# Two pair layers of a 512 x 512 x 128 tensor on one core: three stages of the second layer reordered or repacked

## What is computed

```python
xn = _layernorm(x, ln1_w, ln1_b)
p = _linear(xn, pi_w, pi_b)
g = jax.nn.sigmoid(_linear(xn, gi_w, gi_b))
h = p * g * mask[..., None]
a1, b1, a2, b2 = jnp.split(h, 4, axis=-1)
x1 = jnp.einsum('bikd,bjkd->bijd', a1, b1)
x2 = jnp.einsum('bkid,bkjd->bijd', a2, b2)
y = jnp.concatenate([x1, x2], axis=-1)
yn = _layernorm(y, ln2_w, ln2_b)
return _linear(yn, po_w, po_b) * jax.nn.sigmoid(_linear(yn, go_w, go_b))
```

## Time and profile before

| | us |
|---|---|
| median of the runs | 6269.43 |
| profiled execution | 6311.94 |
| its span on the core | 6310.3 |
| stage 4, about 1860 to 2775 of the span | 915 |
| stage 5, about 2775 to 4150 | 1375 |
| stage 6, about 4150 to 5259 | 1109 |
| stage 7, 5259.9 to the end | 1050 |

### The profile page before, as it was taken

How to read it: one execution, slowest core, us unless ns; L and a number is a source line. 1 busy time by engine, 2 the same in 40 slices (tenths; PEclk the granted TensorE clock), 3 DMA queues, 4 the chain that set the end, 5 groups by cost and what they waited for, 6 DMA issues and landing times. The chain is left out here.

```text
span 6310.3 us, 102506 instructions
## 1 busy us (share of the span) xinstructions
PE 4668.6 (74%) x29248; PEld 2698.7 (43%) x29248; DVE 4518.2 (72%) x6294; ACT 3638.4 (58%) x5197; POOL 2859.0 (45%) x1817
## 2 busy tenths in 40 slices
PE   0016656557539999968888888878887776999999
PEld 0015555543215555544444444445542233555554
DVE  5877767763657777777777777756666666777777
ACT  0017777762227766656666666645554455777777
POOL 0003333320017777756666666642223323666666
PEclk9998888988769999989999999999998888999999
DMA  7967777878739999977777777665555546999998
GB/s 295 366 226 174 187 172 175 181 177 285 242 128 348 345 343 339 342 252 251 249 249 249 247 250 249 238 213 199 199 195 185 180 160 227 326 324 327 325 325 307
DMA packets 991497, 1585.60 MB, mean 251 GB/s; under 512 B 40608, under 2 KB 403040, under 8 KB 988896
## 3 DMA queue, kind: packets, MB, share of 16 engines
q1 hardware_dynamic: 851488, 1398.78, 69.2%
q10 hardware_dynamic: 135680, 167.79, 7.3%
q0 software_dynamic: 4160, 16.78, 0.8%
HBM read 1060.48 MB, written 522.72 MB: 251 GB/s over the span
## 5 line engine op out<-in xcount | busy, mean ns | idle before, releaser
L1231 PE MATMUL s_y_ps<-s_ab 128*128 128x512 f16 x3072 | 747.4, 402 | 200.6 <-DVE s_ab L1287 142.7
L1509 POOL TENSOR_TENSOR s_oT<-s_gated,s_x1t 128x512 f32<-128x512 f32 x512 | 650.9, 1271 | 489.2 <-DVE s_gated L1438 487.3
L410 POOL TENSOR_TENSOR s_low<-s_xh,s_high 128x512 f16<-128x512 f32 x256 | 344.6, 1346 | 1042.4 <-DVE s_high L406 1042.4
L937 POOL TENSOR_TENSOR s_low<-s_xc,s_high 128x1024 f16<-128x1024 f32 x256 | 546.0, 2133 | 516.6 <-ACT s_high L900 516.1
L799 POOL TENSOR_TENSOR s_x1T<-s_gz,s_xT 128x512 f32<-128x512 f32 x512 | 650.2, 1270 | 233.4 <-DVE s_gz L765 231.2
L368 PE MATMUL s_turned_ps<-k_ident,s_xt 128*128 128x128 f32 x2048 | 366.1, 310 | 296.7 <-DMA s_xt<-in_x 259.1
L1231 PEld LDWEIGHTS s_y_ps<-s_ab 128*128 128x128 f16 x3072 | 309.9, 103 | 593.8 <-issue 278.5
L1008 DVE SCALAR_TENSOR_TENSOR s_h<-s_p_ps,k_pi_bias,s_gate 128x1024 f32<-128x1024 f32 x256 | 328.3, 1283 | 306.9 <-ACT s_gate L905 287.2
L706 PE MATMUL s_g_ps<-s_xT,s_Wg 128*128 128x512 f32 x1024 | 523.8, 593 | 0.0
L765 DVE SCALAR_TENSOR_TENSOR s_gz<-s_z_ps,k_z_bias,s_g 128x512 f32<-128x512 f32 x512 | 384.5, 751 | 192.3 <-ACT s_g L732 190.0
L900 ACT ACTIVATE s_high<-s_xc 128x1024 f16<-128x1024 f32 x256 | 270.6, 1057 | 420.1 <-DVE s_xc L1001 419.9
(11 more groups left out here) (209 smaller groups left out, 12712.4 us busy)
## 6 DMA issues: line engine op xcount, KB each, us to landing
s_xt<-in_x SPq DMA_DIRECT2D x512, 512.0 KB, 11.1
x_d<-s_x1T SPq DMA_DIRECT2D x128, 1024.0 KB, 9.1
s_xt<-x_d SPq DMA_DIRECT2D x128, 1024.0 KB, 8.3
h_d<-s_h SPq DMA_DIRECT2D x128, 1024.0 KB, 6.4
s_x1t<-x_d SPq DMA_DIRECT2D x256, 512.0 KB, 5.3
out<-s_ot ACTq DMA_DIRECT2D x256, 512.0 KB, 5.5
s_bt<-b_d SPq DMA_DIRECT2D x64, 1024.0 KB, 9.9
s_mask_b<-mask_d SPq DMA_DIRECT2D x128, 512.0 KB, 4.3
```

What stands on the lines that cost most here:

```text
L410: engine.tensor_tensor(low[:, u % 8, :], xh[:, u % 4, :], high[:, u % 8, :], ALU.subtract).then_inc(rest_ready[u % 2], 1)
L937: pool.tensor_tensor(low[:, n % 4, :, :], xc[:, n % 4, :, :], high[:, n % 4, :, :], ALU.subtract).then_inc(rest_ready, 1)
L1231: last = pe.matmul(y_ps[:, ib, 0:N], ab[:, u % 2, 0, a, kb, ib * P:(ib + 1) * P], ab[:, u % 2, 1, b, kb, :], start=m == 0, stop=m == len(t ...
L1509: pool.tensor_tensor(oT[:, row % 4, :], gated[:, row % 2, :], x1t[:, row // 2, row % 2, :], ALU.add).then_inc(added, 1)
```

## The change

In stage 5 ScalarE applies the sigmoid of pair n before it rounds pair n+2. In stage 6 the units are dealt out by a table, SLOTS, and stand ahead of the copy and the total of their quarter; the square and its sum of a quarter move behind the units of the next quarter; and the closing computation is cut into four pieces of 512 columns that pass between DVE and ACT, with two float16 parts where there were three bfloat16 ones. In stage 7 a row pair is the unit of everything: each of the two rows is multiplied from its own 64 partitions with 64-row weights, the two interleaved and written to two PSUM banks; gate, mix and addition take 1024 columns in one instruction; loads of x1 and stores move four rows; loads run up to 16 rows ahead; the spread runs four pairs ahead.

```diff
-                    for e in range(2):
-                        own, other = slice(64 * e, 64 * e + 64), slice(64 - 64 * e, 128 - 64 * e)
-                        dve.memset(w[other, :, e, :], 0.0)
...
+                    dve.tensor_copy(w[:, 0, :], wide[:]).then_inc(rounded, 1)
...
                 def step(r, n, last=False):
+                    open_gate(r, n)
                     if not (last and n + 2 >= PAIRS):
                         round_high(r, n + 2)
-                    open_gate(r, n)
...
+    SLOTS = (((), (0, 1, 2, 3), (4, 5, 6), (7,)), ((0,), (1,), (2, 3), ()))
...
-                        if after[0] == 0:
-                            turn(*after, 2 * ib)
-                            turn(*after, 2 * ib + 1)
+                        if after[0] == 0 and ib + 1 < RB:
+                            for v in SLOTS[0][ib + 1]:
+                                turn(*after, v)
...
+                        if after[0] < 2:
+                            for v in SLOTS[after[0]][ib]:
+                                round_high(*after, v)
+                        if ib:
+                            square(n - 1, ib - 1)
                         act.wait_ge(product, n)
                         act.activation(y[:, u, ib, :], y_ps[:, ib, 0:N], ACT.Copy).then_inc(copied, 1)
-                        if after[0] < 2:
-                            for v in range(ib * UNITS[after[0]] // RB, (ib + 1) * UNITS[after[0]] // RB):
-                                round_high(*after, v)
-                        act.wait_ge(summed, n)
-                        act.activation(y_ps[:, ib, 0:N], y_ps[:, ib, 0:N], ACT.Square).then_inc(squared, 1)
+                    square(n, RB - 1)
...
+                        if after[0] < 2:
+                            for v in SLOTS[after[0]][ib]:
+                                rest(*after, v)
+                        if ib:
+                            add_square(n - 1, ib - 1)
                         dve.wait_ge(copied, n)
                         dve.tensor_tensor(total[:, ib, :], total[:, ib, :], y_ps[:, ib, 0:N], ALU.add).then_inc(summed, 1)
...
+                    add_square(n, RB - 1)
...
-                step(dve.reciprocal(total[:], total2[:]))
...
+                    dve.reciprocal(total[:, ib, :], y[:, 1, ib, :]).then_inc(inverted, 1)
...
+                def product(dst, weights, n):
+
+                    for w, part, first, last in ((0, high, True, False), (1, high, False, False), (0, low, False, True)):
+                        for e in range(2):
+                            own = slice(64 * e, 64 * e + 64)
+                            done = pe.matmul(dst[:, e, 0:N], weights[own, w, :], part[own, n % 4, :], start=first, stop=last)
+                    return done
+
+                def project(r, n):
+                    pe.wait_ge(rest_ready, r * PAIRS + (n + 5))
+                    pe.wait_ge(sig, r * PAIRS + (n + 1))
+                    product(g_ps, K.Wgo, n).then_inc(g_done, 1)
+                    pe.wait_ge(mixed, r * PAIRS + (n + 2))
+                    product(p_ps, K.Wpo, n).then_inc(p_done, 1)
...
+                    if not (last and n + 4 >= PAIRS):
+                        scale(r, n + 4)
+                    if not (last and n + 2 >= PAIRS):
+                        mix(r, n + 2)
+                    if not (last and n + 4 >= PAIRS):
+                        rest(r, n + 4)
```

More of the change, by code:

```diff
@@ L1403, in step @@
-                def step(r, row, last=False):
-                    if row % 2 == 0 and not (last and row // 2 + 2 >= PAIRS):
-                        spread_scale(r, row // 2 + 2)
-                    if not (last and row + 2 >= ROWS):
-                        project(r, row + 2)
-                    turn(r, row)
-                spread_scale(0, 0)
-                spread_scale(0, 1)
+                    pe.wait_ge(scaled, r * PAIRS + (n + 1))
+                    pe.matmul(r_ps[:, n % 2, 0:N], K.halves[:], rt[:, n // 2, n % 2, :], start=True, stop=True).then_inc(spread, 1)
@@ L1413, in _ @@
+                for n in range(4):
+                    spread_scale(0, n)
                 project(0, 0)
                 project(0, 1)
[L1415 to L1419 removed]
+                with pe.Fori(0, REPS - 1) as r:
+                    for n in range(PAIRS):
+                        step(r, n)
@@ L1441, in step, with mix @@
-                def step(r, row, last=False):
-                    mix(r, row)
-                    if not (last and row // 2 + 2 >= PAIRS):
-                        (rest if row % 2 else scale)(r, row // 2 + 2)
-                for n in range(2):
+                    dve.tensor_tensor(low[:, n % 4, :], yn[:, n % 4, :], high[:, n % 4, :], ALU.subtract).then_inc(rest_ready, 1)
+                def mix(r, n):
+                    dve.wait_ge(sig, r * PAIRS + (n + 2))
+                    dve.wait_ge(p_done, r * PAIRS + (n + 5))
+                    dve.wait_ge(added, r * PAIRS + (n + 1))
+                    dve.scalar_tensor_tensor(gated[:, n % 4, :, :], p_ps[:], K.po_bias[:], gate[:, n % 2, :, :],
+                                             ALU.add, ALU.mult).then_inc(mixed, 1)
@@ L1447, in _, with step @@
+                def step(r, n, last=False):
+                    if not (last and n + 4 >= PAIRS):
+                        scale(r, n + 4)
+                    if not (last and n + 2 >= PAIRS):
+                        mix(r, n + 2)
+                    if not (last and n + 4 >= PAIRS):
+                        rest(r, n + 4)
+                for n in (0, 2):
                     scale(0, n)
+                    scale(0, n + 1)
                     rest(0, n)
-                with dve.Fori(0, N // ROWS - 1) as r:
-                    for row in range(ROWS):
-                        step(r, row)
@@ new lines, in open_gate, with keep @@
+                def open_gate(r, n):
+                    act.wait_ge(g_done, r * PAIRS + (n + 1))
+                    act.wait_ge(mixed, r * PAIRS + (n + 1))
+                    act.activation(gate[:, n % 2, :, :], g_ps[:], ACT.Sigmoid, bias=K.go_bias[:]).then_inc(sig, 1)
+                def keep(r, n):
+                    if n % 2 == 0:
+                        act.wait_ge(stored[n // 2], r * 16 + 16)
+                    for j in range(2):
+                        act.wait_ge(turned, r * (2 * PAIRS) + (2 * n + j + 9))
+                        act.activation(ot[:, n // 2, 2 * (n % 2) + j, :, :], o_ps[:, j, 0:N].rearrange("p (q c) -> p q c", c=P),
+                                       ACT.Identity).then_inc(kept, 1)
@@ new lines, in store, with step @@
+                def store(r, k):
+                    act.wait_ge(kept, r * (2 * PAIRS) + (U * k + U + 2))
+                    act.dma_start(out_v[:, bass.ds(r * (2 * PAIRS) + U * k, U)], ot[:, k, :, :, :]).then_inc(stored[k], 16)
+                def step(r, n, last=False):
+                    if not (last and n + 2 >= PAIRS):
+                        open_gate(r, n + 2)
+                    if not (last and n + 4 >= PAIRS):
+                        round_high(r, n + 4)
+                    keep(r, n)
+                    if n % 2 == 1:
+                        store(r, n // 2)
@@ new lines, in _ @@
+                with pool.Fori(0, REPS) as r:
+                    for n in range(PAIRS):
+                        if n % 2 == 0:
+                            pool.wait_ge(x_loaded[n // 2], r * 16 + 16)
+                        pool.wait_ge(mixed, r * PAIRS + (n + 3))
+                        pool.wait_ge(turned, r * (2 * PAIRS) + (2 * n + 2))
+                        pool.tensor_tensor(oT[:, n % 4, :, :], gated[:, n % 4, :, :],
+                                           x1t[:, n // 2, 2 * (n % 2):2 * (n % 2) + 2, :], ALU.add).then_inc(added, 1)
```

264 lines of the change are left out of this document (121 added, 143 removed).

## The result

Four runs of the kernel before had a median of 6268.96 us (6258.84 to 6276.66), four of the changed kernel 5655.40 us (5638.74 to 5662.02): 0.902 of before, 95% interval 0.899 to 0.904, or 614 us less. The forecast was 5887 with a range of 5775 to 6000. The direction was right; the gain was 614 us where 382 was forecast, and 5655 lies outside the range.

The account below looks back on a forecast made before the run. It took PE as stage 7's bound and a loop of waits as stage 5's. Savings of 160 + 56 + 98 + 11 + 57 = 382 us took the profiled 6311.94 to 5930, the median 6269 to 5887; range 5775 to 6000.

Parts of the forecast that it names:

- The transfers become the bound: Stage 7: with products overlapped, transfers at 343 GB/s bound it at 985 us plus 8, against 1050 before: -57 us.
- share and rate of stage 4 are a full queue's: Stage 7: reason for taking 343 GB/s as the transfer limit, from stage 4's share of 1.05 at that rate.
- the rival to which 0.05 was given: Stage 7: transfers have no ceiling at 343 GB/s with two queues; engines' 3.2 us a pair, 5724 us in all; chance 0.05.
- the 2.8 worked out: Stage 7: PE's time in us for a row pair if products on different halves of the rows run together.
- the slower rival: Stage 7: granted clock could fall to 1.2 GHz, halves one after the other, 7.4 us a pair, 6799 in all; chance 0.04.
- The forecast's 0.2 to 0.3: Stage 7: further us a pair by the rule that changing tiling mode drains TensorE, giving 3.1, still below the transfers' 3.84.
- These two wait for each other once a pair: Stage 5: DVE (3.91) and PE (3.94) wait for each other, so a pair takes 4.15 us; the stage -160 us.
- I keep 7.6: Stage 5: extras in a turn of 16 pairs, table loads and a variance, go from 8.2 to 7.6 us.
- PE's own sum is 15.84 - 1.82 = 14.0: Stage 6, first half: PE's wait of 1.82 us a channel goes and nothing takes its place, -56 us.
- That makes 14.0, against 17.2: Stage 6, second half: DVE becomes the bound, a channel takes 14.0 us instead of 17.2, -98 us.
- The rival of crowded remainders: Stage 6, second half: DVE and POOL slow each other, a channel has limit 15.9, 5945 us in all; chance 0.10.
- The end of the stage: End of stage 6: pieces let ACT's square and root run beside DVE, 30.6 us becomes 20, -11 us.

## Why the prediction was wrong

**The step that failed** is the one of stage 7: "The transfers become the bound: 338.4 MB now, 0.5 less with two parts for three, at 343 GB/s". From it followed 985 us and -57. Stage 7 carried 403 GB/s and took 850. The reason given, "share and rate of stage 4 are a full queue's with the same 2 KB rows", read the share as a measure of what is left. It isn't one here. A share of 0.97 stood beside 338 and 340 GB/s while the engines were the bound, 1.02 beside 347, and 1.05 beside 342, 385, 399 and 403. So the 0.96 at 325 of the earlier trace rows did not stand against the rival either. Stage 4's 343 was no ceiling of its traffic either, since 385 went through once the x loads had a second queue and an earlier issue. What cost the one queue its rate, narrow z loads between the others, the wait ahead of each issue, or both, is open: earlier issue on one queue gave 362 and left PE waiting for z, and the run without z can be read in two ways. Stage 7 alone showed at most 10 us from the second queue and 27 from the size of transfers.

What happened is close to the rival to which 0.05 was given, "stage 7 goes to its engines' 3.2". The engines' loop measured 3.09 with fewer loads and the pair 3.25 with all. That took 197 us instead of 57, 140 of the 268 us by which the profiled gain of 650 passed the forecast 382. At 403 GB/s the transfers do begin to count: PE waits 88 us for s_rt, and fewer bytes gave 40 us. The page "DMA: Bandwidth & Descriptors" of the Trainium skill, section Specifications, which was put against the forecast with a fabric ceiling of 435 GB/s, agrees with this trace so far that 403 lies below it. I had weighed the page against one row and took the row for a limit without asking what else in stage 4 could hold it. Two smaller slips don't move the forecast: 325 / 0.96 is 338.5, not 337, and POOL's addition of 1024 columns took 2.70 us where at most 2.54 was allowed.

**The packing itself** was right: halves run together, 0.66 us for six products where 1.30 stood, and the experiment with full rows lost 160 us. The pair at its shortest, 2.74, is near the 2.8 worked out. The clock stayed at 1.00, 2.4 GHz, with PE busy 88% of the stage, so the slower rival was absent. By the Trainium skill, "TensorEngine Tiling (Array Packing)", section Key Properties, every change of tiling mode drains TensorE. The trace agrees in part. From the spread on four rows to the products it is 0.31 to 0.32 us whether these use 64 rows or 128 (5201.31 to 5201.62, and in the run with full rows by the timeline 5201.94 to 5202.26), but from 64 rows to the transposes on 128 it is about 0.15 longer than from 128 to 128. The forecast's 0.2 to 0.3, for which it gave no working, was somewhat too much. The pair took 2.74 even so, because the 2.8 already held 0.34 of gaps. Whether a drain is the reason of the 0.15 wasn't tried.

**Stage 5** was right in mechanism and too small by 92 us. The gate's wait went (18.9 us left in 1030, where 1.02 stood in each pair), and no wait of that size took its place. The two numbers mis-sized are "These two wait for each other once a pair (transposes for statistics), so I take 4.15", measured 3.91, which is PE's own sum with nothing lost, and "I keep 7.6", measured 5.1. The two engines wait little for each other (PE 51.7 us of 1030 for the statistics); DVE can follow itself at 3.74, which probably lets it catch up. Why the extras fell, from 8.2 to 5.1, was not tried. The swapped lines alone gave all of the gain (1074.1 against 1077.8).

**Stage 6** was right in both halves: "PE's own sum is 15.84 - 1.82 = 14.0" measured 13.87; "That makes 14.0, against 17.2" measured 13.3, with the two stalls of a square seen at 0.65 where 0.75 was taken, and PE's pause 2.1 in the mean, 2.78 at its longest, where 3.6 was. Together -185 for -154. The rival of crowded remainders (15.9) didn't come: the two beside POOL's mask took 2.25 each (2.17 in the earlier trace rows), the others 1.22. The end of the stage gave 13 for 11; the reciprocals, 12.98, kept their length in four pieces.

## What to carry to other kernels

A transfer share near 1 was no proof of a ceiling in these runs, and the GB/s beside it no capacity. Before a rate is carried from one stage to another as a limit, look whether the engines there wait for transfers, and move or take away one stream of that stage to see if the rate is its own. Where each engine works in its written order, first ask of every instruction in the tightest loop who needs it next: here two swapped lines were worth 250 us of 6270. Products that use 64 of TensorE's rows each were worth pairing here, in either written order.

## What the runs showed of the hardware that was not expected

- The share of the transfers stayed between 0.96 and 1.05 while the rate went from 325 to 403 GB/s, and one queue alone carried 399 GB/s.
- Six 64-row products took 0.66 us when three of one half stood ahead of three of the other, 0.66 interleaved and 1.30 on full rows. TensorE started the other half's products before the third of the first half, against the written order.
- From products on 64 rows to transposes on 128 it took about 0.15 us longer than from products on 128.
- Stage 4, the same code in each, took from 834 to 880 us in ten kernels that leave it alone, while in kernels that leave them alone stage 5 by its marks stays between 1074 and 1082, stage 6 between 853.4 and 857.8, stage 7 between 828 and 833. With the x loads on a second queue it was 779.0 and 780.2 in two kernels. What moves it was not tried.
